# A per-token attention, feed-forward and expert kernel: score blocks of four tokens in eight array tiles, and another order of the stages behind them

## The reference

```python
# sublayer 1, on x' = layernorm(x):   (attention "over heads" of the single token)
fq = elu(q) + 1;  fk = elu(k) + 1                    # b h n d
kv  = einsum('bhnd,bhne->bnde', fk, v)               # sums over the heads h, token by token
qkv = einsum('bhnd,bnde->bhne', fq, kv)
qk  = einsum('bhnd,bnd->bhn', fq, fk.sum(over h))
x1  = x' + (qkv / (qk + 1e-6)) @ wo + bo
h   = gelu(layernorm(x1) @ fc_w + fc_b)              # 256 -> 1024
x2  = x + x1 + h @ proj_w + proj_b                   # 1024 -> 256
# sublayer 2, on z = layernorm(x2): two of eight experts, chosen once per batch of 2048 tokens
gates = softmax of the two largest of (z.mean(axis=1) @ gate_w.T + gate_b)
out = x2 + sum over e of gates[e] * gelu(z @ expert_w[e].T + expert_b[e])
```

## Time and profile before

| | |
|---|---|
| median of 3 executions | 1196.86 us (1196.32 to 1197.43) |
| the profiled execution | 1194.7 us, its span 1192.9 |
| PE busy | 1048.4 us, 88%, 8136 matmul records |
| PE weight loads | 779.5 us, 65% (beside PE) |
| DVE busy | 729.8 us, 61% |
| ACT busy | 499.5 us, 42% |
| POOL busy | 178.5 us, 15% |
| mean granted TensorE clock | 0.928 of full |
| mean DMA rate | 101 GB/s |
| chain that ended last | PE 72%, issue 11%, DVE 9% |

### The profile page before, as it was taken

The page is one execution under the profiler, slowest core; times in us unless marked ns, Lnnn a source line. Parts: engine busy times, 40 slices in busy tenths (PEclk is TensorE's granted clock), DMA queues, the critical chain, the costliest instruction groups (busy, mean ns, idle before and its releaser), DMA issues.

```text
span 1192.9 us, 23418 instructions
## 1 busy us (share of the span) xinstructions
PE 1048.4 (88%) x8136; PEld 779.5 (65%) x8136; DVE 729.8 (61%) x1692; ACT 499.5 (42%) x771; POOL 178.5 (15%) x113
## 2 busy tenths in 40 slices
PE   5767989898998899999999899999999896987856
PEld 3445858676777668585867667685868565665623
DVE  2286566666666666766666675766667674645333
ACT  2313444544353444445453545444453433332322
POOL 1021020211111111102021112112020111111000
PEclk9757989999898899999999999999999899998969
DMA  5635343434242443443544344433445434121023
GB/s 178 149 76 122 78 121 79 124 75 123 71 114 77 113 109 95 119 102 93 135 101 118 107 111 106 119 93 105 115 101 138 108 84 97 37 65 68 14 75 106
DMA packets 255833, 119.93 MB, mean 101 GB/s; under 512 B 225168, under 2 KB 241808, under 8 KB 255504
## 3 DMA queue, kind: packets, MB, share of 16 engines
q1 hardware_dynamic: 249104, 108.47, 36.0%
q10 hardware_dynamic: 6656, 10.50, 2.4%
HBM read 60.20 MB, written 58.72 MB: 100 GB/s over the span
## 4 chain that ended last, share of the span: by engine, by line
PE 72%; issue 11%; DVE 9%; POOL 2%; DMA 2%; ACT 2%; DVEq 0%; SPq 0%; ACTq 0%; POOLq 0%
PE pw L959 16%; PE pj L944 15%; PE ps L920 10%; PE ps L902 7%; PE pw L930 5%; PE pw L870 5%; PE pj L870 4%; PE pw L902 3%; DVE am L680 3%; PE ps L1001 3%; PE ps L858 2%; DVE hT L710 1%; POOL x_sb L447 1%; PE pw L910 1%; ACT hidden L526 1%
## 5 line engine op out<-in xcount | busy, mean ns | idle before, releaser
L959 PE MATMUL pw<-hT,w_fc 128*128 128x512 f32 x768 | 212.1, 417 | 30.4 <-DVE hT L710 29.7
L944 PE MATMUL pj<-w_pj,hidden 128*128 128x256 f32 x1536 | 214.1, 289 | 1.4 <-DVE hidden L694 1.4
L694 DVE TENSOR_TENSOR hidden<-xhT,hidden 128x512 fp32r<-128x512 f32 x128 | 88.6, 692 | 201.1 <-ACT hidden L526 201.1
L944 PEld LDWEIGHTS pj<-w_pj,hidden 128*128 128x128 f32 x1536 | 192.3, 189 | 22.5 <-issue 14.9
L525 ACT ACTIVATE xhT<-pw,col 128x512 f32<-128x512 f32 x128 | 88.1, 688 | 279.9 <-PE pw L959 279.3
L959 PEld LDWEIGHTS pw<-hT,w_fc 128*128 128x128 f32 x768 | 144.5, 199 | 66.1 <-DVE hT L710 31.7
L680 DVE TENSOR_TENSOR am<-ps,mask 128x512 f32<-128x512 f32 x256 | 158.9, 684 | 17.6 <-PE ps L920 17.5
L920 PE MATMUL ps<-kq 16*128 16x128 f32 x2048 | 146.9, 438 | 16.0 <-DVE am L680 9.2
L920 PEld LDWEIGHTS ps<-kq 16*128 16x128 f32 x2048 | 128.5, 329 | 42.3 <-issue 33.3
L902 PE MATMUL ps<-xhT,w_qkv 128*128 128x512 f32 x256 | 120.6, 627 | 2.5 <-ACT xhT L478 2.5
L532 ACT ACTIVATE ot<-pw,den_eps 128x512 f32<-128x512 f32 x64 | 81.8, 1278 | 49.6 <-PE pw L930 49.6
(11 more groups left out here) (109 smaller groups left out, 1165.0 us busy)
## 6 DMA issues: line engine op xcount, KB each, us to landing
scratch_nd<-ot SPq DMA_DIRECT2D x32, 512.0 KB, 4.1
nd<-scratch_nd SPq DMA_DIRECT2D x96, 128.0 KB, 2.6
x_sb<-in_x SPq DMA_DIRECT2D x16, 512.0 KB, 4.6
scratch_v<-feat_v ACTq DMA_DIRECT2D x16, 512.0 KB, 2.8
scratch_q<-fqk SPq DMA_DIRECT2D x32, 256.0 KB, 2.7
...
vd<-scratch_v SPq DMA_DIRECT2D x128, 64.0 KB, 2.7
kq<-scratch_q SPq DMA_DIRECT2D x128, 64.0 KB, 2.5
```

Source lines behind the costliest of these rows:

```text
L694: nc.vector.tensor_tensor(hidden[:, m % SLOTS, 1], gelub[:, u], hidden[:, m % SLOTS, 0].bitcast(f32), ALU.subtract).then_inc(S["rest_ready ...
L944: last = nc.tensor.matmul(pj[u][:, D * s:D * (s + 1)], hidden[:, m % SLOTS, a, lo:lo + P], w_pj[:, b, m], start=(m == 0 and n == 0 and s = ...
L959: last = nc.tensor.matmul(pw[bank], w_fc[:, b, c, P * m:P * (m + 1)], hT[:, a, c], start=(n == 0), stop=(n == len(order) - 1))
```

## The change

Scores and weighted sums work in blocks of 4 tokens x 16 heads = 64 columns. The two halves v of 64 array columns (scores) or array rows (weighted sums) times the four groups j give eight array tiles. One call now covers half the tile's tokens: 8 x 2 x 4 = 64 matmuls (128 records), and there are two calls per tile instead of four: scores(0) in `B0`, scores(1) in `M2`, weighted(0) in `M1`, weighted(1) in `M3`. The result is in `sa[0]` and `sa[1]`, so `pw[0]` and `pw[1]` alternate for `up`. `am` has one buffer, and its semaphore `am_used` goes. ACT copies `ot` behind the gelu of m = 1 and ahead of that of m = 5, two copies each. `vd` is loaded in 16 transfers with runs of 128 bytes, q and k are stored with runs of 128 bytes.

In the order: `K0` moves ahead of `M1`, `K1` ahead of `DS`, `N0` ahead of `M4`. `D2` is split in `DV`, `DQ` and `DK`, and `A2` stands between `DV` and `DQ`; its result is now in the banks `sb`. `H` moves from behind `B0` to between `F1` and `F3`, and F1's banks become `sb`.

```diff
-TB = 4
+TB = 2
 TA = 2 * TB
-GG = QT // TA
-RG = 4
-HG = GG // 2
-ROUNDS = GG // RG
+BLOCK = TA * H
+KG = HALF // (2 * TA)
+ROUNDS = 4
...
-FULL = ["L", "XS", "VL", "M1", "K0", "J2", "Y", "M2", "DS", "M3", "Z", "D1", "K1", "M4", "N0", "XL", "X", "J7", "JA", "YB", "E", "VT", "N", "D2", "A2",
-        "F1", "R", "F3", "F4", "SA", "B0", "H", "FX", "F2"]
-HEAD = ["L", "XS", "VL", "M1", "K0", "J2", "Y", "M2", "DS", "M3", "Z", "D1", "K1", "M4", "N0", "XL", "E", "X", "J7", "JA", "YB", "G", "VT", "N", "D2", "A2",
-        "F1", "R", "F3", "F4", "SA", "B0", "H", "FX", "F2"]
+FULL = ["L", "XS", "VL", "K0", "M1", "J2", "Y", "M2", "K1", "DS", "M3", "Z", "D1", "N0", "M4", "XL", "X", "J7", "JA", "YB", "E", "VT", "N", "DV", "A2",
+        "DQ", "R", "DK", "F1", "H", "F3", "F4", "SA", "B0", "FX", "F2"]
+HEAD = ["L", "XS", "VL", "K0", "M1", "J2", "Y", "M2", "K1", "DS", "M3", "Z", "D1", "N0", "M4", "XL", "E", "X", "J7", "JA", "YB", "G", "VT", "N", "DV", "A2",
+        "DQ", "R", "DK", "F1", "H", "F3", "F4", "SA", "B0", "FX", "F2"]
...
         c, b = {
-            "pw_full0": (r == 0, 0), "pw_free0": (r == 0, 1), "pw_full1": (1 + (r > 0), 0), "pw_free1": (1 + (r > 0), 0),
-            "rest_ready": (2, 0), "am_used": (0, 1), "sc_full": (0, r < ROUNDS - 1), "sc_free": (0, r < ROUNDS - 1),
+            "pw_full0": (1, 0), "pw_free0": (1, 0), "pw_full1": (1, 0), "pw_free1": (1, 0), "rest_ready": (2, 0),
+            "sa_full0": (0, r % 2 == 0), "sa_free0": (0, r % 2 == 0), "sa_full1": (0, r % 2 == 0), "sa_free1": (0, r % 2 == 0),
+            "sc_full": (0, r == 1), "sc_free": (0, r == 1),
...
-                    for n, c in enumerate("qk"):
+                if p.stage in ("DQ", "DK"):
+
+                    for n, c in ((0, "q"),) if p.stage == "DQ" else ((1, "k"),):
                         for m in range(NC):
-                            wait("f_ready", at("f_ready", NC * n + m + 1))
+                            wait("f_ready", at("f_ready", m + 1))
                             sp.dma_start(qk_dram[n][p.t % 2].rearrange("u (c p) t -> c p u t", p=P)[m],
-                                         fqk[:, NC * n + m].rearrange("p (u t) -> p u t", t=HALF)
...
-                    src = v_dram.rearrange("(h d) (j b t) -> j b d h t", d=HD, j=NQ, b=2)
+                    src = v_dram.rearrange("(h d) (j b v t) -> j b v d h t", d=HD, j=NQ, b=2, v=2)
                     for j in range(NQ):
                         for b in range(2):
-                            sp.dma_start(vd[2 * j + b::2 * NQ].rearrange("p (h t) -> p h t", h=H), src[j, b]).then_inc(S["v_in"], 16)
+                            for v in range(2):
+                                sp.dma_start(vd[2 * j + b::2 * NQ].rearrange("p (v h t) -> p v h t", v=2, h=H)[:, v],
+                                             src[j, b, v]).then_inc(S["v_in"], 16)
...
-                    wait("pw_free0", at("pw_free0", 1))
+                    for u in range(2):
+                        wait(f"sa_free{u}", at(f"sa_free{u}"))
                     sp.dma_start(nd_dram.rearrange("j e h t -> (j e) h t")[:, :, part], ot[:, :, part]).then_inc(S["nd_out"], 16)
...
+                        if "B" in parts and r % 2 == 0 and u == int(r == 0):
+                            dst = ot[:, :, :].rearrange("p h (b v a k) -> p b v k h a", b=2, v=2, k=KG)
+                            for v in range(2):
+                                wait(f"sa_full{v}", at(f"sa_full{v}", 1))
+                                src = sa[v].rearrange("p (k h a) -> p k h a", k=KG, h=H)
+                                nc.scalar.activation(dst[:, r // 2, v], src, ACT.Identity,
...
-                def masked(r):
+                def masked():
 
                     wait("sc_full", at("sc_full", 1))
-                    wait("am_used", at("am_used"))
                     for j in range(NQ):
-                        last = nc.vector.tensor_tensor(am[:, r % 2, j].rearrange("p (g n) -> p g n", n=P),
-                                                       ps[:, j].rearrange("p (g n) -> p g n", n=P),
-                                                       mask[:, :].unsqueeze(1).broadcast_to([P, RG, P]), ALU.mult)
+                        last = nc.vector.tensor_tensor(am[:, j].rearrange("p (k n) -> p k n", n=BLOCK),
+                                                       ps[:, j].rearrange("p (k n) -> p k n", n=BLOCK),
+                                                       mask[:, 0:BLOCK].unsqueeze(1).broadcast_to([P, KG, BLOCK]), ALU.mult)
                     last.then_inc(S["sc_free"], 1)
...
+                    for u in range(2):
+                        if "C" in parts:
+                            m = 2 * r + u
+                            wait(f"pw_free{u}", at(f"pw_free{u}", 1))
+                            nc.vector.tensor_tensor(hidden[:, m % SLOTS, 1], gelub[:, u], hidden[:, m % SLOTS, 0].bitcast(f32),
+                                                    ALU.subtract).then_inc(S["rest_ready"], 1)
+                        if "B" in parts and r == 1 and u == 0:
+                            masked()
...
-                    for j in (4, 5, 0, 1, 2, 3):
+                    for j in range(*PARTS[p.stage]):
...
-                def scores(r):
+                def scores(b):
 
                     wait("sc_free", at("sc_free"))
-                    for g in range(RG):
-                        at_g = slice(RG * (r % 2) + g, P * HG, HG)
-                        for j in range(NQ):
-                            rows = slice(32 * j, 32 * j + HD)
-                            last = nc.tensor.matmul(ps[:, j, P * g:P * (g + 1)], kd[rows, r // 2, at_g], qd[rows, r // 2, at_g],
-                                                    start=True, stop=True)
+                    for k in range(KG):
+                        for v in range(2):
+                            for j in range(NQ):
+                                rows = slice(32 * j, 32 * j + HD)
+                                cols = slice(BLOCK * KG * v + k, BLOCK * KG * (v + 1), KG)
+                                last = nc.tensor.matmul(ps[BLOCK * v:BLOCK * (v + 1), j, BLOCK * k:BLOCK * (k + 1)],
+                                                        kd[rows, b, cols], qd[rows, b, cols], start=True, stop=True)
                     last.then_inc(S["sc_full"], 1)
 
-                def weighted(r):
+                def weighted(b):
 
                     wait("sc_free", at("sc_free"))
-                    wait("pw_free0", at("pw_free0", up_in_w))
-                    for g in range(RG):
-                        for j in range(NQ):
-                            last = nc.tensor.matmul(pw[0][32 * j:32 * j + 32, P * g:P * (g + 1)], vb[:, GG * j + RG * r + g],
-                                                    am[:, r % 2, j, P * g:P * (g + 1)], start=True, stop=True)
-                    last.then_inc(S["am_used"], 1)
+                    pe.sem_inc(held, 1)
+                    for k in range(KG):
+                        for v in range(2):
+                            rows = slice(BLOCK * v, BLOCK * (v + 1))
+                            cols = slice(BLOCK * k, BLOCK * (k + 1))
+                            for j in range(NQ):
+                                last = nc.tensor.matmul(sa[v][32 * j:32 * j + 32, cols], vb[rows, KG * (2 * j + b) + k],
+                                                        am[rows, j, cols], start=True, stop=True)
+                            if k == KG - 1:
+                                last.then_inc(S[f"sa_full{v}"], 1)
...
-                    up_in_w = int("C" in parts and r == 0)
                     if "C" in parts:
                         up(2 * r)
-                        if r == 0:
-                            up(1)
-                    if "B" in parts and r < ROUNDS - 1:
-                        if r + 1 == ROUNDS // 2:
-                            wait("kq_in1", at("kq_in1"))
-                        scores(r + 1)
+                    if "B" in parts and r == 1:
+                        empty("sa")
+                        wait("kq_in1", at("kq_in1"))
+                        scores(1)
                     if "C" in parts and r:
                         wait("rest_ready", at("rest_ready"))
                         down(2 * r - 1)
+                    if "B" in parts and r == 2:
+                        weighted(1)
+                    if "C" in parts:
                         up(2 * r + 1)
-                    if "B" in parts:
-                        weighted(r)
+                    if "B" in parts and r == 0:
+                        empty("sa")
+                        empty("pw")
+                        weighted(0)
...
-                                    last = nc.tensor.matmul(sa[u][:, D * s:D * (s + 1)], attnT[:, a, c, lo:lo + P],
+                                    last = nc.tensor.matmul(sb2[u][:, D * s:D * (s + 1)], attnT[:, a, c, lo:lo + P],
...
```

(2 more changed lines are left out.)

133 lines of the change are left out of this document (57 added, 76 removed), and 3 rows, old and new, of the table INC.

## The result

The changed kernel takes 1265.07 us (1254.46 to 1273.62), 1.054 times the kernel before (95% interval 1.048 to 1.061). It is slower by 68, where 1170 was forecast. The profiled execution took 1265.31, its span is 1263.4.

What follows compares the result with a forecast made beforehand. TensorE (PE) was taken as the bound, moving to SP's queue after the change. Full tiles +12, heads +2, tiles without experts -26, others -4, -3, -8 sum to -27 on 1194.7: 1168, as median 1170; range 1140 to 1215.

Steps and rivals of the forecast that it cites:

- The blocks: On PE: a new scores block takes 2.3 us, a weighted one 1.0; gain 6.5 us a tile.
- the floor of 32 ns a record: Rival on PE: each small matmul record costs 32 ns, blocks 4.1 us; tiles don't pay, 1205 to 1215, chance 0.25.
- The `vd` loads and SP's chain: SP's queue: 16 loads take 10.6 us, delay everything behind them, and SP's queue becomes the bound.
- The rival of stretched landings: DMA: 128-byte runs make landings (4.17 and 3.80) a third longer; 1215 or more, chance 0.10.
- The first division: On DVE ahead of M4: `rest` queues behind it, so PE stalls 6.9 us ahead of `down` 6.
- `attnT` at +44.4: End of the second division on DVE: `nd` issued +36.0, reciprocal +39.8, `attnT` +44.4 us from the first `up`.
- The hole ahead of the first `up` that should go: On PE: the 2.16 us wait for the split of the transposed input disappears, because the transposes come earlier.
- The back half: On PE from the output projection to the next first `up`: 20.9 us, plus 0.7 for the clock.
- its 66.0: Full tile with experts, first `up` to first `up`: 66.0 us against 63.96 before; six such tiles add 12.
- the wrong rivals: Alternatives: tiles don't pay 0.25, transfers stretch 0.10, cheaper `vd` loads 0.14, hole stays or something unseen 0.06.
- The signs that were to refute the prediction: In a full tile: `nd` issued before +23, blocks taking 4 us, or landings over 5 us.
- the signs that were to confirm it: Full tile: blocks 2.3 and 1.0, hole about 7 before `down` 6, loads 10 to 11, `attnT` near +44, no first-`up` hole.

Runs made afterwards that it cites:

- `after_three`: Changed kernel with first division back behind the fourth round, POOL's additions held until attnT, 115 never executed words ahead of the full-tile loop: 1191.9 us, 0.996.
- `after_three_vdm`: `after_three` with v stored so that 8 loads instead of 16 fill vd, the store in two parts: 1129.9 us, 0.947.
- `yb_late`: Changed kernel with POOL's two additions of row vectors held until attnT is written: 1210.8 us, 1.012.
- `blocks_dead`: Changed kernel with the old order of stages, plus 115 never executed instruction words in an untaken branch of PE: 1142.7 us, 0.955.
- `blocks_vdm`: `blocks_dead` with 8 vd loads instead of 16 and the store of v in two parts: 1122.1 us, 0.938.
- `hybrid`: `blocks_vdm` with the new order (first division behind M4, POOL held) in start-up tiles and tiles without experts only: 1110.8 us, 0.927.

## Why the prediction was wrong

1. **The blocks** were right. Forecast 2.3 and 1.0, measured 2.35 and 1.42. In the scores block records start 18 ns apart, in the weighted one 11 ns, so the floor of 32 ns a record doesn't hold for eight array tiles side by side. Nor does the 25 ns that the Trainium skill ("TensorE: Matmul & The Clock Gate", section "Back-to-back issue gap") states for one matmul behind another: the measurement decides. The weighted sum was undersized by 0.4; the gain is 5.5 a tile, not 6.5. The blocks alone gave -39, with 16 loads.

2. **The `vd` loads and SP's chain**: the term was near (10.6 forecast, 12.5 measured in the full tile, 10.5 in `after_three`; first `nd` forecast at +25.8 and issued at +24.1, the second at +36.0 and +35.8). That SP's queue becomes a bound was right, and `after_three_vdm` shows its worth, 62 with the landings in it, but in the changed kernel, with the other parts in, eight loads give 27. The rival of stretched landings fell there: 4.18 and 4.15 from `ot` to `nd`.

3. **The first division**: the mechanism was right, the stall smaller (2.59 against 6.9 in the full tile), because PE reached `down` 6 later than forecast, at +31.2 and not +26.0; it went on at +33.8, forecast +32.9. In tiles without experts I counted none; it is 2.5 there, where the division also stands behind two normalisations on DVE. Its removal is worth 52: the stall delays `down` 7, that the residual's addition, and that the second division and POOL's additions together, so that they meet.

4. **The failed step is `attnT` at +44.4.** I took 3.80 from the issue of `nd` to the reciprocal, and 4.55 from there to `attnT`, as fixed from rows of before and never read POOL's timeline. Measured are 4.74, because the second division came behind the residual's addition, which `down` 7 releases, and 7.35, because its products met POOL's additions: +47.9. In the kernel before, the reciprocal began 4.2 us behind the residual's addition, and the products 1.2 us behind POOL's. `yb_late` prices the meeting with POOL at 54.

5. **A cost that had no term**: PE's code. The sum counted time per instruction and not that a loop body of 1587 words a pass instead of some 1070, by the trace's count, has to be kept somewhere. The hole ahead of the first `up` that should go did lose its cause: the waits for the split of the transposed input fell from 29.7 to 3.6 us. But 27.8 us of "issue" came in their place, with a granted clock of 0.50 at the first `up` of the full tile shown. Shifting the body is worth 15 in the old order; in the changed kernel it takes 18.5 off the six inner full tiles in sum. The Trainium skill ("Runtime: NRT & Kernel Launch", section "Instruction fetch mechanics") gives 2048 instructions in blocks of 256 for PE; the body is shorter than that and was loaded again all the same. Counted in such blocks from the start of PE's program, branches not taken included, it lay in eight of them, in seven after the shift. The loop without experts, 1521 words a pass, lies in seven, and its second and third pass load nothing. That eight are one too many fits every run (101 or 102 loads with the one place, 64 or 66 with the other) but is an inference, since no record names what is dropped.

6. **The back half**: 20.9 and 0.7 for the clock forecast, 27.0 measured: 4.3 of code holes, 1.3 of clock in the projection. Of the 9.0 us by which the full tile missed its 66.0, 3.5 lie in `attnT` and 5.4 here. The design's order, above all queries and keys behind the projection, costs 45 with the old blocks and 49 with the new ones (`after_three` against `blocks_dead`), but only 8 once SP has eight loads (`after_three_vdm` against `blocks_vdm`), in both pairs with POOL held on the side of the new order. That 8 is a sum of two signs: the six inner full tiles lose 23, the tiles without experts gain 8, and the three heads gain 7, in which `hybrid` kept the old order; the new one there and not in the full tiles was not run.

The forecast's 1170 lies near what the blocks give in the old order (1158 to 1143), but not by its own sum; what was costed too kindly is the order. The range's upper end came from the wrong rivals: what happened, an interlock of DVE's queue, POOL and `attnT`, and code that is loaded again, was not among them. The signs that were to refute the prediction were not the right ones either: in the full tile shown `nd` was not issued before +23, the blocks didn't take 4, the landings were 3.9 to 4.2 and not over 5, and yet the forecast was off by 95 us. Of the signs that were to confirm it, two failed, `attnT` near +44 and no hole ahead of the first `up`, and the stall of 7 came as 2.6.
